# Second stage of a three-part vision block: a mask, sums, a product and two elementwise steps change their place in the engines' orders

## What is computed

```python
# h: (64, 64, 192), result of the token stage; _ln: layer norm
x  = _layernorm(h)
xn = _ln(x)
k, v, q = (xn @ W.T + 0.1 * modifier(xn) for W in (Wk, Wv, Wq))   # modifier: 192 -> 48 -> 768 with gelu
k, v, q = (_ln(a.reshape(b, s, 12, 64)) for a in (k, v, q))       # per head
def step(M, kvq):                                                 # scan over the 64 positions
    out_t = M q_t
    kn = k_t / (norm(k_t) + 1e-6)
    pred = M kn
    M_new = M - outer(pred + lr * (pred - v_t), kn)
h = h + sigmoid(x @ Wg.T + bg) * (outs @ Wo.T)
f = relu(_layernorm(h) @ W1.T + b1) @ W2.T + b2
h = h + _layernorm(f @ Wo2.T + bo)
```

## Time and profile before

| What | Value |
|---|---|
| Runs | 1354.27, 1350.39, 1351.59 us; median 1351.59 |
| Profiled execution | 1347.21 us, span of its instructions 1345.2 us |
| TensorE clock granted, mean | 0.969 (1.00 in the windows from 540 to 1240 us) |
| Busy share of the span | PE 92%, weight loads 73%, VectorE 64%, ScalarE 46%, GpSimd 40% |
| Second stage, 840 to 940 us | PE 95.06, weight loads 82.12, VectorE 82.32, ScalarE 60.16, GpSimd 63.17 us busy of 100 |
| ScalarE, squares of 768 columns (L910) | 845 ns, mean of 96 |
| Chain that ended last, whole span | PE 32%, issue 29%, GpSimd 27%, VectorE 6% |

### The profile page before, as it was taken

One profiled execution on the slowest core, in us unless ns is written; L12 is line 12 of the kernel. 1 busy time (PEld: TensorE's weight loads), 2 busy tenths in 40 slices (PEclk: granted clock), 3 DMA queues, 4 the chain that ended last, 5 costly groups with the idle time before them and its releaser, 6 DMA issues.

```text
span 1345.2 us, 44929 instructions
## 1 busy us (share of the span) xinstructions
PE 1231.8 (92%) x17572; PEld 988.4 (73%) x17572; DVE 858.4 (64%) x2184; ACT 614.7 (46%) x1539; POOL 542.5 (40%) x689
## 2 busy tenths in 40 slices
PE   5898999999997579999999999999999999999975
PEld 5865666666664468888888888888888887888774
DVE  0137433333333368878887888888788878888762
ACT  0012222222222355656665666656566656665532
POOL 0000000000000356566646665665566466656631
PEclk8999999999998689999999999999999999999987
DMA  9888999999991012112212221221122122211210
GB/s 326 300 327 325 381 379 372 374 375 373 376 376 37 18 22 50 32 37 50 38 35 39 46 38 35 40 47 35 36 45 44 32 38 50 38 35 35 47 32 15
DMA packets 219992, 179.22 MB, mean 133 GB/s; under 512 B 164342, under 2 KB 189881, under 8 KB 219321
## 3 DMA queue, kind: packets, MB, share of 16 engines
q1 hardware_dynamic: 219818, 176.79, 41.2%
HBM read 154.72 MB, written 22.02 MB: 131 GB/s over the span
## 4 chain that ended last, share of the span: by engine, by line
PE 32%; issue 29%; POOL 27%; DVE 6%; SPq 2%; DMA 2%; ACT 1%; POOLq 0%; DVEq 0%; ACTq 0%
PE PS L438 28%; POOL region L1110 9%; POOL region L1093 5%; POOL region L1098 3%; POOL region L1076 2%; POOL region L1104 2%; POOL region L1088 1%; PE PS L514 1%; SPq L308 1%; POOL region L1083 1%; POOL region L1060 1%; SPq L398 1%; PE PS L692 1%; PE PS L532 1%; PE PS L599 1%
## 5 line engine op out<-in xcount | busy, mean ns | idle before, releaser
L438 PE MATMUL PS<-region 64*64 64x64 f32 (+6 forms) x5864 | 351.6, 286 | 19.9 <-DVE region L1158 12.7
L438 PEld LDWEIGHTS PS<-region 64*64 64x64 f32 (+3 forms) x5864 | 230.1, 139 | 114.9 <-issue 105.0
L1110 POOL TENSOR_TENSOR region<-region,powers 128x12 f32<-128x12 f32 x96 | 224.2, 2336 | 7.5
L905 ACT ACTIVATE region<-PS 128x512 f32<-128x512 f32 (+1 forms) x192 | 93.3, 486 | 187.1 <-PE PS L438 187.1
L1039 POOL TENSOR_TENSOR region<-region,powers 128x1 f32<-128x1 f32 x32 | 6.1, 189 | 404.2 <-DVE region L1218 404.2
L692 PEld LDWEIGHTS PS<-region 64*64 64x64 f32 x4608 | 145.6, 138 | 22.9 <-issue 18.9
L692 PE MATMUL PS<-region 64*64 64x64 f32 x4608 | 158.4, 223 | 1.4 <-ACT region L938 1.4
L438 PE MATMUL PS<-cw_hi,xr_hi 128*128 128x512 f32 (+3 forms) x384 | 148.5, 387 | 1.9 <-ACT region L905 1.4
L438 PE MATMUL PS<-cw_lo,xr_hi 128*128 128x512 f32 (+3 forms) x384 | 130.6, 340 | 0.0
L438 PE MATMUL PS<-cw_hi,xr_lo 128*128 128x512 f32 (+3 forms) x384 | 130.2, 339 | 0.0
L1351 DVE TENSOR_TENSOR region<-region 128x768 f32<-128x768 f32 x96 | 102.8, 1072 | 39.2 <-POOL region L1110 38.9
(11 more groups left out here) (170 smaller groups left out, 2280.0 us busy)
## 6 DMA issues: line engine op xcount, KB each, us to landing
region<-in_Wq SPq DMA_DIRECT2D x32, 1152.0 KB, 6.3
region<-in_Wk SPq DMA_DIRECT2D x32, 1152.0 KB, 8.6
region<-in_Wv SPq DMA_DIRECT2D x32, 1152.0 KB, 7.8
region<-in_x SPq DMA_DIRECT2D x32, 384.0 KB, 7.4
n_scratch<-region SPq DMA_DIRECT2D x64, 192.0 KB, 3.3
region<-h_scratch SPq DMA_DIRECT2D x64, 96.0 KB, 2.0
region<-in_w SPq DMA_DIRECT2D x2, 2304.0 KB, 13.2
region<-i_scratch SPq DMA_DIRECT2D x256, 12.0 KB, 1.8
```

Source lines behind the costliest of these rows:

```text
L438: return nc.tensor.matmul(dst, lhsT, rhs, start=first, stop=last)
L905: act.activation(raw[:, col:col + width], PS[:, PIECE_BANK[i], 0:width], ACT.Copy).then_inc(S["raw_ready"], 1)
L1110: pool.tensor_tensor(rs[:, cols], rs_var[:, cols], root[:, cols], ALU.pow).then_inc(S["rs_ready"], 1)
```

## The change

In words: on VectorE the mask of E (`take_e`) goes ahead of the sums, all three sums of a tile (`moments(t, 0..2)`) now stand in the tile's own step t, the third one after the two scalings of k and q, and `scale(j, 2)` and `high_part(x)` leave the engine. ScalarE gets both: v's scaling as 12 ACTIVATE instructions of 64 columns behind `take_piece(t, 0)`, the high part as one ACTIVATE behind `gelu(x)`; its `squares(t, 2)` moves up, ahead of `take_z`. GpSimd makes the three head scales in order, all in the tile's own step. TensorE issues `ffn_second` one step later, behind the 12 transposes of `turn_kq`, and without its wait for `gated_ready`.

```diff
@@ TensorE
             def ffn_second(l):
                 pe.wait_ge(S["f1_ready"], l + 1)
                 need(pe, "raw_ready", upto(l + 3, 6))
-                pe.wait_ge(S["gated_ready"], l + 1)
                 mm(PS[:, 7, 0:ATT], f1[:, :], ffn2[:, :]).then_inc(S["f2_mm"], 1)
...
                 if live(j):
                     turn_kq(j)
+                if live(m):
+                    ffn_second(m)
                 if live(l):
                     read_out(l)
...
                 if live(l):
                     ffn_first(l)
-                    ffn_second(l)
@@ ScalarE
+            def high_part(x):
+                act.wait_ge(S["mod_ready"], 3 * x + 3)
+                act.wait_ge(S["xlin_copied"], 2 * x + 2)
+                need(act, "piece_mm", 6 * (x - 1))
+                need(act, "xr_ready", x - 1)
+                act.activation(xr_hi[x % 2][:, :, :], x_aug[:, :, :], ACT.Copy).then_inc(S["xr_hi"], 1)
+
+            def scale_v(j):
+                act.wait_ge(S["rs_ready"], 3 * j + 3)
+                act.wait_ge(S["raw_ready"], 6 * j + 6)
+                need(act, "rscale_ready", j - 1)
+                for h in range(HEADS):
+                    last = act.activation(vs[j % 2][:, h * HD:(h + 1) * HD], raw[:, 2 * KD + h * HD:2 * KD + (h + 1) * HD], ACT.Copy,
+                                          scale=rs[:, 2 * HEADS + h:2 * HEADS + h + 1])
+                last.then_inc(S["vs_ready"], 1)
...
                 if live(t):
                     take_piece(t, 0)
+                if live(j):
+                    scale_v(j)
                 if live(t):
                     take_piece(t, 1)
...
                 if live(x):
                     gelu(x)
+                    high_part(x)
...
                 if live(t):
                     take_piece(t, 5)
+                    squares(t, 2)
...
                     copy_y2(l)
-                if live(t):
-                    squares(t, 2)
@@ GpSimd
                 if live(l):
                     residual_rstd(l)
-                if live(j):
-                    head_rstds(j, 2)
+                if live(t):
+                    head_rstds(t, 0)
                 if live(m):
                     output_rstd(m)
                 if live(t):
-                    head_rstds(t, 0)
                     head_rstds(t, 1)
+                    head_rstds(t, 2)
                 if live(l):
                     shifted_residual(l)
@@ VectorE
                 if live(j):
-                    moments(j, 2)
                     take_norm(j)
...
-                if live(t):
-                    moments(t, 0)
                 if live(k):
                     take_e(k, 0)
                     take_e(k, 1)
+                if live(t):
+                    moments(t, 0)
+                    moments(t, 1)
                 if live(l):
                     norm_h2(l)
+                if live(x):
+                    low_part(x)
                 if live(j):
-                    scale(j, 2)
                     right_side(j)
-                if live(t):
-                    moments(t, 1)
-                if live(x):
-                    high_part(x)
-                    low_part(x)
...
                 if live(t):
                     scale(t, 0)
                     scale(t, 1)
+                    moments(t, 2)
                 if live(j):
                     invert_small(j)
```

More of the change, by code:

```diff
@@ L767, in ffn_second @@
                 need(pe, "raw_ready", upto(l + 3, 6))
-                pe.wait_ge(S["gated_ready"], l + 1)
                 mm(PS[:, 7, 0:ATT], f1[:, :], ffn2[:, :]).then_inc(S["f2_mm"], 1)
             for s in range(TILES + 5):
-                x, t, j, k, l = s, s - 1, s - 2, s - 3, s - 4
+                x, t, j, k, l, m = s, s - 1, s - 2, s - 3, s - 4, s - 5
                 if live(j):
                     turn_kq(j)
+                if live(m):
+                    ffn_second(m)
                 if live(l):
@@ L1344, in scale @@
                 dve.wait_ge(S["rs_ready"], 3 * t + m + 1)
[L1345 to L1351, removed]
+                need(dve, "kqT_mm", 3 * t)
+                dve.tensor_tensor(kq[:, m * KD:(m + 1) * KD].rearrange("p (g d) -> p g d", d=HD),
                                   raw[:, m * KD:(m + 1) * KD].rearrange("p (g d) -> p g d", d=HD),
                                   rs[:, m * HEADS:(m + 1) * HEADS].unsqueeze(2).to_broadcast([P, HEADS, HD]), ALU.mult)\
-                   .then_inc(S["kq_ready" if m < 2 else "vs_ready"], 1)
+                   .then_inc(S["kq_ready"], 1)
             def take_e(k, i):
@@ L1452, in normalise @@
                 dve.tensor_scalar(xh[:, :], xn[:, :], rstd_parts[:, 5:6], None, ALU.mult).then_inc(S["xh_ready"], 1)
[L1454 to L1458, removed]
             def low_part(x):
```

## The result

| | before | changed |
|---|---|---|
| Median of the runs | 1351.71 us | 1340.89 us |
| Ratio, 95% interval | | 0.9936 [0.9917, 0.9955] |
| Profiled execution, span | 1347.21, 1345.2 us | 1343.92, 1342.0 us |
| Period, mean of 25 full steps (`key_lengths`, 4th to 29th) | 26.49 us | 26.14 us |

Faster, as forecast, and inside the range (1320 to 1350), but about half of the 17 us: by the ratio 0.64% of 1351.7 is 8.7 us (6 to 11); the difference of the two medians, 10.8 us, lies within that. The two profiled spans differ by only 3.2 us, because the first stage, which the change does not touch, took 4.4 us longer in the second one: GpSimd's first `input_rstds` starts at 443.47 before and 447.89 after. From there to the end it is 901.7 against 894.1 us, 7.6 faster: 8.8 in the 25 full steps, 0.9 lost ahead of them and 0.3 behind them.

A forecast was written before the change was run, and what follows sets the result against it. Bound: VectorE and GpSimd alternating, PE following. 0.6 us off each of 25 periods (15 us) plus 2 us at the ends took profiled 1347.2 to 1330; 4.4 us above that, a median of 1334 us, range 1320 to 1350.

The forecast's parts named there:

- the contention with the inversion: VectorE's inversion beside v's power and the shifted residual: 0 to 0.4 us lost each step, taken as 0.25.
- q's power: On GpSimd, ready between 828.6 and 829.6 us, taken as 828.85, against 830.15 before.
- the ends: Some three steps at either end of the second stage: about 0.3 us gained in each, 2 us together.
- The mask: On VectorE, ahead of k's sums: PE may start y 0.86 us earlier, no gain yet; the sums start 0.93 later.
- ScalarE's part: v's scaling as 12 ScalarE instructions: 3.2 us inside the 4.76 us hole ahead of take_piece(t, 1), costing nothing.
- VectorE's relief: 1.3 us a step taken off VectorE: worth nothing by itself, since VectorE waits for the power for q anyway.
- The product behind the transposes: ffn_second on PE: its 0.46 us wait only moves to the transposes; small gain, some 0.15 us on PE.
- PE's floor: The period PE needs by itself: 25.53 us less 0.15, so 25.4 us.
- B: Rival: PE takes over as bound, the loop wanting 25.4 us a period; 29 us faster, 1322 us; chance 0.17.
- C: Rival: nothing moves; q's add and power fall behind result's instructions, inversion loses 0.4 us; 1351 within 4; chance 0.09.
- D: Rival: scale(t, 0) on VectorE gets in ahead of GpSimd's power for q; period 27.1 us, 1368 us; chance 0.12.
- E: Rival: v's power on GpSimd holds VectorE's inversion for its whole 2.28 us; period 28.2 us, 1394 us; chance 0.04.

The follow-up runs named there:

- b_mask: Kernel before, with only the mask of E put ahead of the sums of k on VectorE: median 1351.8 us, ratio 1.0006, period 26.52 us.
- b_ffn: Kernel before, with only the second FFN product moved behind the next key transposes, without its wait for gated_ready: median 1351.2 us, ratio 1.0002.
- a_resid: Changed kernel, GpSimd's shifted residual moved to behind the residual's power, its output double-buffered: median 1330.0 us, ratio 0.9842 to the kernel before.
- a_both: a_resid, with GpSimd's final norm's power also moved ahead of k's: median 1319.1 us, ratio 0.9762 to the kernel before.
- a_sums: Changed kernel, with only the sums of k put back ahead of the mask of E: median 1331.5 us, ratio 0.9876 to the kernel before.
- a_vdve: Changed kernel, with v's scaling back on VectorE as one multiply ahead of the right side: median 1357.1 us, ratio 1.0054 to the kernel before.
- a_late: Changed kernel, turn_kq waiting for the relu and y2's copy only where that bank is written: median 1338.7 us, ratio 0.9927 to the kernel before.
- a_both_late: a_both with the turn_kq edit of a_late: median 1305.3 us, ratio 0.9678 to the kernel before.

## Why the prediction was right and wrong

The direction, the bound and the part that gives the gain were right; the size was not. Of the 17 us forecast 7.6 came in the profiled stage. Three terms of the sum were mis-sized, each by about 3 us: the contention with the inversion, the time at which q's power is ready, and the ends.

*What bounds the kernel: right.* A loop of VectorE and GpSimd in turn, with PE behind it. b_mask and b_ffn moved PE's two gaps without effect, a_resid and a_both moved only GpSimd instructions and gave 0.36 and 0.45 us a period more. VectorE does wait for PE too, 0.94 us ahead of `take_a` in each of these steps, but it waits for GpSimd's `key_lengths` right behind that (2.25 us in the step above), so that wait is not on the loop.

*The mask: right as a permission, and its price was right too.* The idle time of 2.07 us ahead of k's power was in the sum. a_sums shows 0.29 us of it as a net cost.

*Contention with the inversion: mis-sized.* The step of the prediction that failed is "I take 0.25": between 0 and 0.4 it is 0.37 us, nearly the full price, and the add of the shifted residual pays all of it, since a_resid takes it away with that instruction. The row of the 1.34 us multiply stood at hand, and I had no reason to go below it: both times an add of the same size runs whole beside a multiply. 25 x 0.12 is 3 us.

*q's power: 0.1 us late.* I had it ready at 828.85 in the step of before. Put back by the 2.35 us between the two clocks, 831.29 is 828.94: it was issued 0.14 us after the start of `result`'s first multiply and took 2.41 us instead of 2.28. I had taken it that `result` "cannot be in its way early". The row of 2.32 us at 827.83 already had the same meeting. With it the inversion starts 0.73 us earlier and not 0.85: again 3 us in 25 steps. So 0.60 us a period became 0.36.

*The ends: wrong sign ahead of the full steps.* I gave 2 us for the steps at either end; they lost 1.2 us. The largest loss is in the second of the first steps, 24.32 instead of 23.40 us. VectorE in it, before and then changed (the steps start with `input_rstds` at 498.01 and 502.76):

```profile
513.86 0.96 DVE L1351 TENSOR_TENSOR region<-region 128x768 f32<-128x768 f32 x1 [0.64 <-POOL region L1110]
514.74 0.15 DVE L1298 TENSOR_TENSOR region<-region 96x4 f32<-96x4 f32 x1
```

```profile
518.69 0.96 DVE L1364 TENSOR_TENSOR region<-region 128x768 f32<-128x768 f32 x1 [2.16 <-POOL region L1128]
...
520.43 0.15 DVE L1316 TENSOR_TENSOR region<-region 96x4 f32<-96x4 f32 x1
```

There is no tile in phases l and m yet, so GpSimd has fewer powers to make. q's scaling starts 15.85 us into the step before and 15.93 after: taking v's power away gives nothing there, since GpSimd then idles 3.05 us for the sums of k. The sums of v then come on top, and the inversion starts 0.94 us later. The last three steps did gain, 2.0 us, and the stretch behind them lost 2.3 at a lower granted clock; that stretch was not in my sum at all.

*The median.* I put it 4.4 us above the profiled execution, as before; this time the profiled execution was the slowest, 3.0 us above the median. By the median alone the forecast therefore looks nearer (1334 against 1340.89) than by the profiled execution (1330 against 1343.92), and that is luck.

*ScalarE's part: right in time and place* (12 instructions in 2.97 us against 3.2; the hole ahead of `take_piece` is 1.92 us after it). By the formula of the Trainium skill (ScalarE: Activation LUTs, What ACT_TABLE_LOAD costs) it was an estimated 3.0 us. The trace agrees with its 2.97.

*VectorE's relief "is worth nothing by itself": wrong, without effect on the number.* a_vdve lost 0.49 us a period. I counted VectorE's idle time against the length of the multiply, and not what the multiply pushes onto GpSimd's one-column power. In the sum the gain was there without a name: my 0.85 to 1.40 us for the final norm, measured 1.02, is what it takes when the multiply no longer stands beside it.

*The product behind the transposes: right*, shown by b_ffn and, from the other side, by a_late and a_both_late. PE's floor of 25.4 us was right for that order (25.33 in a_both), but it is not PE's work alone: it holds the wait for the relu, and without it the period was 24.84.

*Rivals.* B (PE takes over) did not happen in the changed kernel and did two edits later, at the period named. C came half true: the inversion lost 0.37 of its 0.4 us, and q's power fell behind one instruction of `result`, but its add did not. The result lies about midway between C and the forecast, which 0.09 for C did not suggest. D did not occur: the add for q's power ran ahead of `result`'s first multiply, and the power lost 0.13 us, not a whole scaling. E did not either: v's power ran from 833.52 to 835.79 beside the small multiplies of the inversion, none of which took longer.

By the Trainium skill (SBUF — State Buffer, SBUF: two separate sides) whichever of the two engines starts first has the shared port pair for the whole instruction. The trace agrees for two of GpSimd's instructions and not for its powers of 12 columns. One is the shifted residual (0.34 to 0.39 us lost on VectorE). The other is `scaled_mask`; this is the step above, GpSimd and VectorE, and then the same VectorE instruction alone, near the end of the kernel before:

```profile
819.71 1.47 POOL L1116 TENSOR_TENSOR region<-cst,region 128x768 f32<-128x768 f32 x1 [0.96 <-DVE region L1437]
```

```profile
819.92 1.47 DVE L1384 TENSOR_TENSOR region<-region 128x192 f32<-128x192 f32 x1
```

```profile
1312.67 0.36 DVE L1371 TENSOR_TENSOR region<-region 128x192 f32<-128x192 f32 x1
```

The residual's add takes 1.47 us instead of 0.36. It stands between the gate and the residual's power, in the turn of the two engines, so `scaled_mask` costs up to 1.1 us a step there, three times what the change gained. No run moved it.

## What to carry to other kernels

When two engines hand work to each other in turn, add up one whole turn from start to start before believing a busy share: here PE at 95% was the follower, and emptying its gaps gave nothing until 1.2 us had been taken out of the period by the other two. In such a turn look for instructions whose result is not needed within it (v's power, the shifted residual) and put them where that engine idles and the other one does not read two operands from the same memory. An edit that wins nothing while another engine binds can be worth 0.8% later (a_late and a_both_late), so it is worth trying again each time the bound moves.

## What was not expected of the hardware

A power of 12 columns on GpSimd takes 2.28 us. If a VectorE instruction with two operands in SBUF is running when it is issued, it ends 2.13 us after the end of that instruction (2.41, 2.50 and 2.72 us in the runs above, 2.86 in the earlier trace rows). Sums running at that time do not delay it (the power at 825.26 before took 2.28, with VectorE's sums of q running from 825.03), and a VectorE multiply that starts after it runs at its usual 0.95 us. That fits a collision of its read alone, so that what a power loses depends on which instruction is in flight at its start; only these durations show it. With an add of 192 columns (0.59 us) it is the other side that pays, 0.34 to 0.39 us. These collisions of less than a microsecond, not engine time, put a_sums and a_vdve outside the periods that I had expected.
